# A transformer kernel of four sub-layers: another order of the last part's steps, a semaphore for each dispatched token tile, and another scratch for squares

## The reference

```python
x = x + L0_xattn(layernorm(x), ctx)      # cross-attention, self-attention over 1024 tokens, gelu MLP (1024 wide),
                                         # each with residual, layer norm, gain and bias
x = x + L0_ffn(layernorm(x))             # mixture of 8 experts (256 wide), top 2 by sigmoid, relu squared
x = x + L1_xattn(layernorm(x), ctx)      # cross-attention with 10 prefix keys and a mask
x = x + L1_ffn(layernorm(x))             # ternary weights plus a low-rank part: proj(relu(fc(x))**2)
```

## Time and profile before

| what | us |
|---|---|
| median of 3 runs | 1131.09 |
| lowest, highest | 1127.72, 1136.28 |
| the profiled execution | 1130.95 |
| its span in the trace | 1129.2 |
| busy: TensorE, VectorE, ScalarE, GpSimd | 1021.5, 785.3, 610.2, 330.5 |
| mean granted clock of TensorE, of full speed | 0.958 |

### The profile page before, as it was taken

How to read it: one execution, slowest core, us unless ns; L and a number is a source line. 1 busy time by engine, 2 the same in 40 slices (tenths; PEclk the granted TensorE clock), 3 DMA queues, 4 the chain that set the end, 5 groups by cost and what they waited for, 6 DMA issues and landing times.

```text
span 1129.2 us, 20786 instructions
## 1 busy us (share of the span) xinstructions
PE 1021.5 (90%) x7648; PEld 603.3 (53%) x7648; DVE 785.3 (70%) x1337; ACT 610.2 (54%) x1191; POOL 330.5 (29%) x724
## 2 busy tenths in 40 slices
PE   4899979939999999999997998949899999999997
PEld 2675656413333333333334656626687776576764
...
GB/s 206 64 15 90 44 83 101 103 150 62 46 72 76 46 69 76 46 71 72 37 32 244 6 33 19 10 84 10 62 176 134 122 53 45 33 29 1 20 10 29
DMA packets 97746, 75.68 MB, mean 67 GB/s; under 512 B 49890, under 2 KB 87663, under 8 KB 97391
## 3 DMA queue, kind: packets, MB, share of 16 engines
...
...
## 4 chain that ended last, share of the span: by engine, by line
PE 67%; DVE 10%; DMA 8%; SPq 4%; ACT 4%; issue 3%; POOL 3%; DVEq 0%; POOLq 0%; ACTq 0%
PE TR L843 16%; PE OUT L843 14%; PE OUT L1073 10%; PE TR L849 8%; PE TR L1062 8%; DMA head_q<-MT 5%; PE OUT L1062 4%; SPq L644 3%; PE TR L919 2%; PE SCR L903 2%; SPq L732 2%; DVE small L1459 1%; ACT PTS L1283 1%; PE SCR L896 1%; POOL dispatched L2004 1%
## 5 line engine op out<-in xcount | busy, mean ns | idle before, releaser
L1528 DVE TENSOR_REDUCE small<-SCR 128x1 f32<-128x1024 f32 x256 | 308.7, 1223 | 35.1 <-PE SCR L950 29.1
L1373 ACT ACTIVATE shared<-TR 128x512 f32<-128x512 f32 x321 | 184.9, 597 | 39.9 <-PE TR L1062 33.8
L950 PE MATMUL SCR<-head_k,head_q 48*128 48x512 f32 x512 | 196.2, 461 | 5.2 <-issue 5.2
L1073 PE MATMUL OUT<-shared,HM 128*32 128x256 f32 x2048 | 166.7, 397 | 1.3 <-ACT shared L1373 0.4
L1062 PE MATMUL TR<-head_q,head_k 51*128 51x512 f32 x321 | 135.0, 453 | 18.5 <-DMA head_q<-MT 18.3
L1887 POOL TENSOR_SCALAR small<-small 128x1 f32<-128x1 f32 x112 | 27.8, 248 | 368.0 <-DVE small L1460 366.0
L1373 ACT ACTIVATE shared<-OUT 128x512 f32<-128x512 f32 x191 | 114.2, 598 | 22.6 <-PE OUT L1062 18.2
L843 PE MATMUL TR<-xT,fifo 128*128 128x512 f32 x224 | 108.6, 643 | 1.5 <-ACT xT L1261 1.5
L1062 PEld LDWEIGHTS TR<-head_q,head_k 51*128 51x128 f32 x321 | 55.6, 188 | 82.8 <-issue 31.0
L1073 PEld LDWEIGHTS OUT<-shared,HM 128*32 128x32 f32 x2048 | 41.5, 108 | 94.2 <-ACT shared L1373 56.4
L1283 ACT ACTIVATE PTS<-TR 96x512 f32<-96x512 f32 x128 | 69.8, 589 | 39.3 <-PE TR L849 38.8
...
## 6 DMA issues: line engine op xcount, KB each, us to landing
...
```

The costliest lines, as they stand in the source:

```text
L950: ins = nc.tensor.matmul(SQ[kt % 2][:, hf, :], QX[n % 2][rows, kt * 128:(kt + 1) * 128], KX[n % 2][rows, hf * 512:(hf + 1) * 512], start=T ...
L1073: ins = nc.tensor.matmul(PV[32 * g:32 * g + 32, 0:256], VH[:, n % 2, kt, :], PTB[:, kt % 2, g * 256:(g + 1) * 256], start=(kt == 0), stop= ...
L1373: nc.scalar.activation(PTB[:, kt % 2, hf * 512:(hf + 1) * 512], ring_bank("t_scores", n, kt, hf), ACT.Exp, scale=DH ** -0.5).then_inc(st_d ...
L1528: nc.vector.tensor_reduce(nm[:, n % 2, kt:kt + 1], SQ[kt % 2].rearrange("p h n -> p (h n)"), AX, ALU.max, negate=True).then_inc(sq_done.se ...
```

## The change

1. d_disp becomes a list of 16 semaphores, one for each token tile. DS.t counts up its own. FM.t for t of 8 or more waits for the one of tile t - 8. The first XL of a batch waits for the eight of the batch.
2. SQB[1], the scratch of the odd squares in FC, moves from TOKM (which DM and L3 use) to the first quarter of xT2 (which TOKN uses).
3. ORDER_C is written anew: the same steps in another order. The first line of each side stands for it:

```diff
 ORDER_C = """
-ST.0 RS.0 ST.2 RS.2 SO.0 SO.2 RS.3 RS.1 ST.1 SN.0 SN.2 ST.3 SO.3 LD.4 LD.7 SO.1 RS.7 OL.2 ST.5 LD.5 LX.0 RS.4 RF.0
+ST.0 ST.1 VW.0 RS.0 RS.1 SO.0 RS.3 SO.1 SN.0 RS.2 ST.2 ST.3 SO.3 SN.1 SO.2 LX.0 SN.3 LX.1 ST.4 RF.1 LD.5 LX.3 ST.5
...
-        SQB = [v[:, :, :].rearrange("p r d -> p (r d)") for v in (HB, TOKM)]
+        SQB = [HB[:, :, :].rearrange("p r d -> p (r d)"), xT2[:, 0, 0, :]]
...
-        d_disp = [sem(f"dispatched_{b}") for b in range(B)]
+        d_disp = [sem(f"dispatched_{t}") for t in range(T)]
...
                 def load_dispatched(i):
 
-                    sp.wait_ge(d_disp[i // NS], 16 * 2 * TB)
+                    if min(range(i // NS * NS, (i // NS + 1) * NS), key=lambda j: order_c.index(("XL", j))) == i:
+                        for t in range(i // NS * TB, (i // NS + 1) * TB):
+                            sp.wait_ge(d_disp[t], 32)
...
                     if t >= TB:
-                        dve.wait_ge(d_disp[0], 16 * 2 * TB)
+                        dve.wait_ge(d_disp[t - TB], 32)
...
-                        TOKN[:, t % TB, :], None).then_inc(d_disp[t // TB], 16)
+                        TOKN[:, t % TB, :], None).then_inc(d_disp[t], 16)
```

More of the change, by code:

```diff
@@ L147 @@
[L147 to L151, removed]
@@ new lines @@
+LD.7 RF.3 LD.4 ST.6 SN.2 LX.2 RF.0 RS.4 FI.0 RS.7 RS.5 LD.6 FO.1 SO.5 RS.6 FN.1 OL.2 FO.0 SO.4 SN.5 ST.9 SN.4 RF.2
+ST.7 FO.3 LX.5 FN.0 FO.2 ST.8 OL.3 SO.7 SO.6 LD.10 ST.11 LD.9 SN.7 SN.6 LX.7 LX.4 FM.0 FN.2 FN.3 RF.5 RF.4 LX.6 RS.10
+RS.9 LD.8 FM.2 L2.0 FI.1 RT.0 FM.3 FM.1 FO.5 RS.8 SO.9 RF.7 FN.5 FO.4 SO.8 FN.4 L2.2 L2.1 RF.6 FM.5 LD.13 RT.2 SN.9
+FM.4 SN.8 FO.7 FO.6 LD.11 ST.10 ST.13 SO.10 LX.8 RF.8 RT.1 FN.6 L2.3 RS.11 L2.4 FN.7 ST.14 LD.12 SO.11 RT.3 L2.5 ST.15
+RT.5 FM.7 RS.13 FM.6 SN.11 SN.10 LD.15 LD.14 L2.7 LX.9 RT.7 RT.4 LX.11 ST.12 RF.9 RF.11 L2.6 RS.14 RS.15 RS.12 LX.10
@@ new lines @@
+RT.6 GT.0 FI.2 RK.0 RF.10 FO.9 DS.7 SO.13 FN.9 FO.8 DS.0 SO.12 FN.8 DS.1 FO.10 SN.12 SN.13 FO.11 SO.14 SO.15 FM.9 DS.4
+DS.2 LX.12 LX.13 RF.13 SN.14 DS.3 SN.15 FM.8 L2.9 FN.10 RT.9 LX.14 LX.15 DS.5 FM.10 DS.6 FN.11 XL.3 FM.11 XL.1 XL.0
+L2.8 FI.3 RF.12 RT.8 RF.14 L2.10 XT.0 XL.2 RF.15 FO.13 UP.0 XT.1 FN.13 FO.12 UP.1 L2.11 FN.12 FO.15 XT.2 RT.10 HT.0
+UP.2 DN.0 FN.15 FM.12 FO.14 XT.3 HT.1 XL.5 RT.11 FM.13 XL.4 XT.4 FM.15 UP.3 HT.2 L2.13 DN.1 UP.4 YS.0 XL.6 RT.13 XL.8
+XT.5 YS.1 XL.7 L2.12 FN.14 DN.2 HT.3 XT.6 UP.5 L2.15 HT.4 FM.14 XL.9 DN.3 UP.6 RT.12 L2.14 YS.2 RT.15 RT.14 DN.4 GT.1
@@ new lines @@
+XT.7 HT.5 UP.7 HT.6 XT.8 YS.3 XT.9 XL.10 YS.4 XL.12 UP.8 XL.13 DN.5 DN.6 RK.1 YS.5 HT.7 XL.11 YS.6 XT.10 UP.9 DS.15
+XL.14 HT.8 XT.11 DN.7 UP.10 HT.9 DS.13 XT.12 DN.8 UP.11 XL.16 YS.7 XL.15 DN.9 YS.8 HT.10 UP.12 XT.13 DN.10 YS.9 DS.8
+XT.14 HT.11 UP.13 DS.14 HT.12 UP.14 YS.10 XT.15 XL.17 DN.11 HT.13 YS.11 XT.16 UP.15 XL.18 DN.12 DS.10 DN.13 HT.14
+XT.17 YS.12 UP.16 XL.19 XT.18 YS.13 XL.20 HT.15 DS.9 UP.17 DS.12 XL.21 XT.19 DN.14 DN.15 YS.14 HT.16 UP.18 HT.17 XT.20
+DS.11 DN.16 YS.15 UP.19 DN.17 XL.22 XT.21 YS.16 YS.17 HT.18 UP.20 XL.23 DN.18 XT.22 XL.24 HT.19 UP.21 XL.26 DN.19
@@ new lines @@
+HT.34 QP.0 DM.5 CG.7 RX.5 XL.37 DN.34 UP.36 YS.33 XL.38 S.0 XT.37 HT.35 XT.38 UP.37 XL.39 L3.5 HT.36 E.0 CB.4 UP.38
+XT.39 RX.0 XL.40 S.1 T.0 RX.1 DN.35 YS.34 XT.40 HT.37 YS.35 CB.7 UP.39 DN.36 XL.41 DM.4 PV.0 YS.36 HT.38 DN.37 E.1
+DM.7 RX.2 XT.41 OT.0 S.2 T.1 UP.40 YS.37 CG.6 L3.7 CT.0 XL.42 E.2 DN.38 XT.42 S.3 RX.7 HT.39 PV.1 DN.39 XL.43 L3.4
+XL.44 HT.40 OT.1 T.2 CB.6 PJ.0 DM.6 RX.3 XL.45 YS.39 UP.41 CT.1 PV.2 L3.6 UP.42 YS.38 OT.2 XT.43 HT.41 DN.40 PN.0 PJ.1
+PN.1 UP.43 LT.0 XT.44 DN.41 E.3 HT.42 YS.40 QP.1 XT.45 DN.42 S.4 YS.41 T.3 E.4 UP.44 HT.43 UP.45 CT.2 S.5 PV.3 DN.43
@@ new lines @@
+YS.43 HT.44 RX.4 HT.45 YS.42 RX.6 OT.3 T.4 DN.44 DN.45 PJ.2 YS.44 E.5 PN.2 YS.45 PV.4 CT.3 CG.8 S.6 CG.9 T.5 OT.4 LT.1
+PJ.3 LT.2 PN.3 CB.8 E.6 PV.5 CT.4 CG.10 S.7 LT.3 T.6 CB.9 OT.5 CB.10 DM.8 DM.9 E.7 FC.0 CG.11 PV.6 CG.12 L3.8 PJ.4
+CB.11 L3.9 DM.10 CT.5 OT.6 CG.13 DM.11 T.7 CB.12 FP.0 CG.14 L3.10 PV.7 L3.11 PJ.5 CT.6 QP.2 PN.4 CB.13 DM.12 VW.1
+DM.13 OT.7 CG.15 PJ.6 LT.4 S.8 L3.13 FP.1 E.8 L3.12 FP.3 PN.5 CT.7 S.9 T.8 CB.14 CB.15 PJ.7 DM.14 E.9 RX.8 RX.9 LT.5
+DM.15 PV.8 S.10 T.9 FP.2 L3.14 L3.15 OT.8 E.10 RX.14 PV.9 S.11 RX.15 CT.8 RX.11 QP.3 PN.7 PN.6 RX.13 OT.9 T.10 RX.12
@@ L177 @@
+E.11 S.12 RX.10 PV.10 LT.6 PJ.8 CT.9 PN.8 OT.10 T.11 PJ.9 LT.7 S.13 CT.10 E.12 PV.11 FC.1 LT.8 PJ.10 PN.9 OT.11 T.12
+PN.10 S.14 LT.9 PV.12 E.13 FP.4 CT.11 OT.12 T.13 E.14 PJ.11 FP.6 PV.13 LT.10 PN.11 S.15 CT.12 OT.13 T.14 PJ.12 LT.11
+PV.14 CT.13 FP.5 FP.7 E.15 T.15 PN.12 OT.14 FC.2 PJ.13 CT.14 PV.15 PJ.14 LT.12 OT.15 FP.9 PN.14 CT.15 PN.13 FP.8 PJ.15
+LT.13 PN.15 FP.10 LT.14 LT.15 FP.11 FC.3 FP.13 FP.12 FP.14 FP.15
 """
```

34 lines of the change are left out of this document (5 added, 29 removed).

## The result

The kernel after takes 1122.38 us, median of 20 runs (1117.63 to 1128.60), the kernel before beside it 1130.48 us (20 runs). The ratio is 0.9932, with a 95% interval of 0.9910 to 0.9954: 7.7 us faster by the ratio (8.1 by the two medians), about half of what was forecast. The profiled execution has a span of 1117.8 us.

The account below looks back on a forecast made before the run. TensorE was taken as the bound, busy 1021.5 of 1129.2 us, with gains only at its waits. From 1130.95 us, -12.2 - 1 - 1.7 - 1 - 1.6 + 1.5 = -16.0 gave 1115 us; forecast 1109 to 1120, outer range 1106 to 1124.

Parts of the forecast that it names:

- The dispatch: Before the fourth gelu block: FI.3 no longer waits for all scatters, so XT.0 starts sooner, -12.2 us.
- The scatters beside VectorE: GpSimd's ten last scatter issues beside a busy VectorE: 0 to 4 us more, taken as 0.
- the 1140 us: Rival time if, by the skill page's figure, ten scatter issues take 25 us more; chance 0.05, shared with another rival.
- The second gating: Store YS.1 issued sooner, so TensorE's 3.7 us wait at the gating shrinks: -1.7 us (0 to -3.7).
- the clock: Behind the second gating, 813 to 821 us: a shorter pause avoids the low clock, -1 us (0 to -3).
- The earlier blocks: Waits for norms in front of the FI blocks: -1 us, between -4 and +3.
- VW.1: Second attention: VW.1 comes later behind FC.0, so S.8 is late, +1.5 us (0 to +4).
- the rest of the 300 us behind the gating: Everything else behind the second gating: 0, with 5 us either way.
- my -1.6 for XT.23's load: Later expert tiles: the load for XT.23 is issued first of batch 1, removing its 1.61 us wait, -1.6 us.
- the 5 us more that were to show the prediction wrong: Sign of failure: TensorE's waits behind the second gating grow by more than 5 us in all.
- rival 1: The gain is given back among the experts and in the attention: 1120 to 1130 us, chance 0.20.
- two loads with under 4 us of cover: Argument against rival 1: two such loads in the new order, three before.

Follow-up runs that it names:

- after_fp2: The kernel after with the steps FP.2 and FP.3 exchanged in the order, so that FP.2 takes the other output buffer; 1127.63 us, ratio 0.9898.

## Why the prediction was half right

**The dispatch: right.** Forecast -12.2 from FI.2 to XT.0, measured -10.7. FI.3 came 41.7 us behind FI.2; I had 40.3. VectorE set that, as I had it, but it stood twice for roots on GpSimd, for which I had taken nothing:

```profile
728.03 0.47 DVE L1468 TENSOR_SCALAR HB<-HB,small 128x256 f32<-128x256 f32 x1 [1.06 <-POOL small L1890]
...
738.04 0.41 DVE L1468 TENSOR_SCALAR XN<-XN,small 128x256 f32<-128x256 f32 x1 [0.46 <-POOL small L1890]
```

FI.3 took 15.47 us (taken: 15.8). XT.0 waited 0.29 for its load: the dispatch did end with FI.3, as worked out.

**The scatters beside VectorE: right.** GpSimd in the kernel after, two issues from the middle and the last two:

```profile
728.18 1.08 POOL L2006 DMA_INDIRECT dispatched<-xT,small  x1 [0.18 <-issue]
729.56 1.17 POOL L2006 DMA_INDIRECT dispatched<-xT,small  x1 [0.30 <-issue]
...
751.34 0.96 POOL L2006 DMA_INDIRECT dispatched<-xT,small  x1 [0.31 <-issue]
752.60 0.96 POOL L2006 DMA_INDIRECT dispatched<-xT,small  x1 [0.30 <-issue]
```

The sixteen issues of batch 0 took 0.96 to 1.36 us. VectorE worked 12.3 of the 14.7 us from 727.0 to 741.7, and the last ten issues took 1.03 us in the mean: 0.7 us in all above the 0.96, where I took 0. The Trainium skill, "SBUF — State Buffer", section "A bandwidth-pool intuition that's wrong (but worth ruling out)", gives 3100 ns for a GpSimd DMA beside a VectorE copy. No run here shows anything near it, and the 1140 us worked out from it did not come; no run tells why this case is spared.

**The second gating: right.** -1.7 and -1 for the clock, together -2.7; the stretch lost 2.7 less: TensorE stood 1.7 us less, and the clock gave back 1.2 (0.97 before, 1.00 now). TensorE's wait was 1.77 (2 or less was said), and the clock of 797 to 805 was 1.00 where the earlier trace rows had 0.60. The low clock before went on behind the gating, up to XT.23, so its return was worth 2.2 us more there than the -1. VectorE did the copy before the gating without a wait for a store.

**The earlier blocks: off by 1.7.** -1 was taken, +0.7 came (7.7, 8.3 and 12.9 us lost in front of FI.0, FI.1 and FI.2 became 7.8, 7.8 and 14.0). It lay in the bounds (-4 to +3). VectorE's steps ahead of the last LX were not quite the same ones, as I had it (FM.1 and FM.3 are no longer ahead of FI.1's; FN.10 and RT.9 stand for FN.11 ahead of FI.3's), and TensorE stood 1.5 us longer before FI.2.

**VW.1: wrong, and in its bounds (0 to +4) by luck.** +1.5 was taken, because S.8 would wait. It did not. The stretch lost 3.1 more, and what the runs show of it are two other things: FP.3 on FP.1's buffer (0.8 to 1.4 us, by `after_fp2`) and FC.0's middle (1.0).

**The failing step** is "For the rest of the 300 us behind the gating [...] I take 0, with 5 us either way". It was +2.6 up to XT.23 and +2.0 up to QP.0 (in which my -1.6 for XT.23's load is already counted), some 1.6 behind FC.0 beyond the 1.5, and +1.1 at the end, which is the clock's. Taken together, -1.6 + 1.5 + 0 was forecast behind the gating and +8.8 measured in these stretches, so the term of 0 was 8.9 us, beyond its 5 either way; without the 2.2 us that the clock gave back up to XT.23 it would have been 11. The waits of TensorE behind RK.1 in the list came to 11.0 us before and 15.7 after, at the edge of the 5 us more that were to show the prediction wrong. That is rival 1, to which I gave 0.20. "I found two loads with under 4 us of cover" shows where I looked: at loads alone. Two causes are shown by runs: stores out of turn (YS.18 behind YS.19 and three loads), which VectorE meets two tiles later, worth 2.5 us up to QP.0, and an output buffer used twice in a row, worth about 1 us. Both could be read from the order before any run. The largest piece, up to XT.23, has no shown cause.
